# Tile 7 of a gated attention block: its normalised rows transposed by TensorE and VectorE instead of by two transposing DMAs

## The reference

```python
# x (2,1024,2048), ctx (2,2048,2048), U (2048,512), S (512), V (2048,512)
q(x, s, z) = (clip(round(x / s + z), 0, 255) - z) * s
x = x + tanh(g_xattn) * (q(layernorm(x)) @ q(ctx))
weight = (U * S) @ V.T
x = x + tanh(g_ffn) * einsum('bti,oi->bto', layernorm(x), weight)
```

## Time and profile before

| | us |
|---|---|
| median of 3 runs | 613.83 |
| the profiled execution | 616.85 |
| its span in the trace | 615.0 |
| TensorE busy | 585.1 |
| VectorE busy | 375.7 |
| ScalarE busy | 213.3 |
| GpSimd busy | 191.5 |

### The profile page before, as it was taken

How to read it: one execution, slowest core, us unless ns; L and a number is a source line. 1 busy time by engine, 2 the same in 40 slices (tenths; PEclk the granted TensorE clock), 3 DMA queues, 4 the chain that set the end, 5 groups by cost and what they waited for, 6 DMA issues and landing times.

```text
span 615.0 us, 7436 instructions
## 1 busy us (share of the span) xinstructions
PE 585.1 (95%) x2743; PEld 265.0 (43%) x2772; DVE 375.7 (61%) x694; ACT 213.3 (35%) x258; POOL 191.5 (31%) x148
## 2 busy tenths in 40 slices
PE   2899999999999999999699999999999999999997
PEld 1444444444444444444244444444444444444443
DVE  6849899994397854912363895737466564735212
ACT  5898887723050433345733310302111030301000
POOL 2898740003041438524522910040404021040000
PEclk9999999999999999999799999999999999999999
DMA  8999975539648793889974444091736436181412
GB/s 287 387 387 386 309 210 137 104 121 211 200 108 218 218 206 101 218 231 273 270 214 121 116 69 86 17 210 31 162 95 129 129 73 185 20 169 25 130 51 103
DMA packets 147844, 103.26 MB, mean 168 GB/s; under 512 B 110816, under 2 KB 110816, under 8 KB 147808
## 3 DMA queue, kind: packets, MB, share of 16 engines
q1 hardware_dynamic: 138816, 85.48, 54.0%
q10 hardware_dynamic: 8992, 17.30, 9.0%
HBM read 58.99 MB, written 16.78 MB: 123 GB/s over the span
## 4 chain that ended last, share of the span: by engine, by line
PE 59%; DMA 16%; DVE 13%; issue 4%; SPq 4%; ACT 2%; POOL 1%; ACTq 0%; DVEq 0%
PE bank L527 21%; PE bank L555 12%; DMA v_hl<-in_ctx_dram 7%; PE bank L595 6%; PE bank L600 6%; PE bank L596 6%; PE bank L560 6%; DMA xT<-xs 5%; DMA out_dram<-ring 2%; DVE ring L1067 2%; DVE u_hl L1162 2%; DVE xn L1102 2%; DMA ring<-in_x_dram 1%; DVE xs L1105 1%; DVE v_hl L1156 1%
## 5 line engine op out<-in xcount | busy, mean ns | idle before, releaser
L527 PE MATMUL bank<-q,qT 128*128 128x512 bf16 x873 | 199.1, 381 | 1.6 <-DVE ring L1067 0.3
L527 PEld LDWEIGHTS bank<-q,qT 128*128 128x128 bf16 x896 | 87.7, 98 | 107.8 <-issue 2.6
L555 PE MATMUL bank<-v_hl,xT 128*128 128x512 f16 x512 | 118.5, 386 | 6.9 <-DMA xT<-xs 6.9
L239 POOL TENSOR_SCALAR ring<-ring,bvec 128x2048 f32<-128x2048 f32 x16 | 32.8, 2051 | 271.9 <-DVE bvec L1049 271.9
L244 POOL TENSOR_TENSOR ring<-ring,corr 128x512 f32<-128x512 f32 x64 | 86.5, 1383 | 23.3 <-ACT corr L790 22.3
L595 PE MATMUL bank<-u_hl,hbuf 128*128 128x512 f16 x240 | 91.0, 379 | 2.5 <-ACT hbuf L772 1.3
L596 PE MATMUL bank<-u_hl,hbuf 128*128 128x512 f16 x240 | 91.0, 379 | 0.0
L1120 DVE SCALAR_TENSOR_TENSOR ring<-bank,cy,ring 128x512 f32<-128x512 f32 x64 | 47.3, 746 | 62.4 <-PE bank L600 62.4
L1067 DVE SCALAR_TENSOR_TENSOR ring<-bank,const,ring 128x512 f32<-128x512 f32 x64 | 47.5, 743 | 57.4 <-PE bank L527 55.0
L233 POOL TENSOR_SCALAR q<-u8r,const 128x1024 bf16<-128x1024 uint8 x52 | 64.6, 1250 | 54.6 <-ACT u8r L699 50.9
L555 PEld LDWEIGHTS bank<-v_hl,xT 128*128 128x128 f16 x512 | 50.6, 99 | 69.2 <-DMA xT<-xs 7.9
(11 more groups left out here) (119 smaller groups left out, 455.3 us busy)
## 6 DMA issues: line engine op xcount, KB each, us to landing
out_dram<-ring SPq DMA_DIRECT2D x64, 256.0 KB, 3.7
ring<-in_x_dram SPq DMA_DIRECT2D x62, 256.0 KB, 4.2
v_hl<-in_ctx_dram SPq DMA_DIRECT2D x26, 512.0 KB, 11.6
stage<-in_ctx_dram ACTq DMA_DIRECT2D x22, 512.0 KB, 5.6
q<-in_ctx_dram ACTq DMA_DIRECT2D x10, 512.0 KB, 9.5
u_hl<-in_L_ffn_V_dram SPq DMA_DIRECT2D x8, 512.0 KB, 11.5
stage<-in_ctx_dram SPq DMA_DIRECT2D x6, 512.0 KB, 11.5
stage<-in_L_ffn_U_dram SPq DMA_DIRECT2D x2, 512.0 KB, 5.8
```

Of the source, the lines that this page charges most:

```text
L527: mm = nc.tensor.matmul(unit_bank(t, n)[:, :], qT_of(t)[:, k, :], q2[:, n, k, :], start=(k == 0), stop=(k == KT - 1))
L555: nc.tensor.matmul(h_bank(u)[:, :], xT[:, g, half, k % 8, :], v_hl[:, k, 0, :], start=(g == 0 and a == 0 and half == 0), stop=False)
```

## The change

The rows of tile 7 no longer pass through the two transposing DMAs. TensorE transposes `xs` in 32 pieces of 128x128 against the identity, 8 into each bank, using banks 0 to 2 of `s1` (all of whose blocks of sequence 0 are done by then; bank 0 is used twice). VectorE copies each bank of fp16 into `xT` (`xT_copy`). On ScalarE the second half of the high part moves behind the chunks `CB+13` to `CB+15` and `hT_copy(5)`; on VectorE the second low half moves behind the last two blocks of `mm4(4)`, and `hid_lo(6)` ahead of `y_unit(5, 0)`. SyncE issues the four loads of tile 8 together.

```diff
+    X_PE = TB - 1
+        x_dma = lambda u: u + 1 - (u > X_PE)
+        x_bank = lambda g, half: bank[(2 * g + half) % 3]
...
@@ SyncE
-            load_x(8, 0)
-            x_transpose_half(7, 0)
-            load_x(8, 1)
-            x_transpose_half(7, 1)
-            load_x(8, 2)
-            load_x(8, 3)
+            for n in range(NQ):
+                load_x(8, n)
...
@@ TensorE, mm3
-                    pe.wait_ge(xT_in[g], 16 * (u + 1))
+                    if u == X_PE:
+                        pe.wait_ge(xT_copied, 2 * g + 2)
+                    else:
+                        pe.wait_ge(xT_in[g], 16 * x_dma(u))
...
+            def x_pieces(g):
+                pe.wait_ge(xs_hi, 2 * X_PE + g + 1)
+                pe.wait_ge(xs_lo, 2 * X_PE + g + 1)
+                for half in range(2):
+                    if 2 * g + half < 3:
+                        pe.wait_ge(x1_ready, S1_END(TB - 1) - (2, 1, 0)[2 * g + half])
+                    else:
+                        pe.wait_ge(xT_copied, 1)
+                    dst = x_bank(g, half)[:, :].bitcast(f16)
+                    for k in range(8):
+                        mm = nc.tensor.transpose(dst[:, k * P:(k + 1) * P], xs[:, g, half, k * P:(k + 1) * P], ident_h)
+                    mm.then_inc(xT_written, 1)
...
             h_pieces(5)
+            x_pieces(0)
             mm3(6)
+            x_pieces(1)
             mm4(5)
...
@@ ScalarE
-            x_hi(7)
+            x_hi_half(7, 0)
             stream(13, 16)
             hT_copy(5)
+            x_hi_half(7, 1)
             stream(16, 20)
...
@@ VectorE
+            def xT_copy(g):
+                for half in range(2):
+                    dve.wait_ge(xT_written, 2 * g + half + 1)
+                    dve.wait_ge(mm3_half, 2 * (X_PE - 1) + g + 1)
+                    nc.vector.tensor_copy(xT[:, g, half, :, :].rearrange("p k w -> p (k w)"),
+                                          x_bank(g, half)[:, :].bitcast(f16)).then_inc(xT_copied, 1)
...
             y_unit(4, 1)
-            x_lo_half(7, 1)
             y_unit(4, 2)
             y_unit(4, 3)
+            x_lo_half(7, 1)
+            xT_copy(0)
+            hid_lo(6)
+            xT_copy(1)
             y_unit(5, 0)
-            hid_lo(6)
             y_unit(5, 1)
```

More of the change, by code:

```diff
@@ L123, in gated_block_program @@
         hT_copied = sem("hT_copied")
+        xT_written = sem("xT_written")
+        xT_copied = sem("xT_copied")
         ident_free = sem("ident_free")
@@ L749, in x_hi_half @@
                 act.wait_ge(ln2_ready, u + 1)
-                if u > 0:
-                    act.wait_ge(xT_in[g], 16 * u)
+                if u - 1 == X_PE:
+                    act.wait_ge(xT_written, 2 * g + 2)
+                elif u > 0:
+                    act.wait_ge(xT_in[g], 16 * x_dma(u - 1))
                 nc.scalar.activation(xs[:, g, 0, :], xhalf(u, g), ACT.Identity, bias=bias, scale=scale).then_inc(xs_hi, 1)
```

## The result

The kernel after takes 607.71 us (median of 4 runs, 606.75 to 608.68), the kernel before 614.02 us beside it. The ratio is 0.9897, 95% interval 0.9868 to 0.9926: 6.3 us faster. The forecast was 604.6 us, 603.0 to 608.3, and faster. One execution of the kernel after, taken with the experiments, was slow (1051.23 us, mean granted clock 0.563) and is left out of all medians.

A forecast was written before the change was run, and what follows sets the result against it. TensorE was taken as the bound, stalled in `mm3(7)` by a transposing DMA. Terms -6.5 (stall), -3.0 (half clock), -1.3 (hidden rows), +1.8 (pieces) gave -9.0 to -9.1 us; forecast 604.6 us, range 603.0 to 608.3.

The forecast's parts named there:

- The range: Kernel time: own range 603.0 to 606.2 us with chance 0.72, widened to 608.3 for about 0.85.
- chunks as late as before: Rival: late context chunks delay `hT_copy(6)`, so `mm4(6)` waits 2.3 us; gain 6.8, 607.0 us; chance 0.15.
- The bound and the place: TensorE, 95% busy, waits 6.5 us at L555 in `mm3(7)` for the transposing DMA into `xT`.
- The price of the pieces: On TensorE, 32 added pieces cost 4 x 0.44 = 1.8 us, all on the path.
- The landing L: Landing of context chunk `CB+15`, issued at about 260.1, estimated from the room loads ahead of it: 266.5.
- The copy: VectorE's copy of a bank into `xT`: taken as 1.23 us, between 0.69 and 1.38; bank 7 margin 1.4 us.
- The clock as part of the gain: Second half of `mm3(7)`: its 16 matmuls take 6.42 us at half clock against 3.45, so 3.0 us gained.
- What is late next: `mm4(6)`, due at 296.7, needs `hT_copy(6)`, expected at about 287 instead of 297.95.
- The rival of ScalarE's queue: Part of the 0.15 rival: late `CB+15` delays ScalarE's chain; each us of landing past 267.9 costs one us.
- The sign: Profile after would show about 33.4 us from start of `mm3(6)` to start of `mm4(6)`, against 42.5 before.
- The size: Whole kernel: gain of 9.1 us, taken from the 616.85 us execution and applied to the median 613.83, giving 604.7.
- The DMA rule: By the rule the removed wait would hardly exist; the row had 20.78 us against a median 6.7 for chunk loads.

The follow-up runs named there:

- pieces_twice: Kernel after with each of the 32 transpose pieces made twice; 609.82 us, ratio to before 0.9927.
- fill14: Kernel before with 14 matmuls whose result nobody reads, placed in the stall between the halves of `mm3(7)`; 611.00 us, ratio 0.9972.
- fill26: Kernel before with 26 matmuls whose result nobody reads, placed in the stall of `mm3(7)`; 612.34 us, ratio 0.9977.
- late_half: Kernel after with ScalarE's second high half of tile 7 moved four chunks later, behind `stream(16, 20)`; 614.35 us, ratio to before 1.0011.
- before_again: Kernel before, unchanged, for a second trace and more times; 613.59 us, ratio 0.9981; its traced execution took 613.6 us.
- small_chunks: Kernel before with loads of chunks `CB+15` and `CB+20` to `CB+31` cut to a quarter of their columns, so its result is wrong; 605.48 us, ratio 0.9848.

## Why the prediction was right, and what was off

- **The range** held by luck. The forecast's own range was 603.0 to 606.2, and 607.7 lies outside it. Only the part up to 608.3, which was added for chunks as late as before, reaches it, and that did not happen: `hT_copy(6)` ran at 286.67, and nothing waited in the stretch.
- **The bound and the place** were right. The wait of L555 in `mm3(7)` was the one to remove, and 6.5 us stand in its row before, none after.
- **The price of the pieces**, 4 x 0.44 = 1.8 us on the path, was right: 2 x 0.89 us in the trace, and `pieces_twice` measures the same with twice as many. The 275 ns for a piece that the Trainium skill gives ("TensorE: Matmul & The Clock Gate", section "Part 4: PE-mode transpose") are not the price of a piece here: in a row one follows the other by 56 ns, and the clock stayed at 1.00.
- **The landing L** was put at 266.5 and came at 266.15, but the way to it was not right. It was counted from the last room load, landing at 264.5, and 1.5 us for one load more. In the trace after, the last of these, issued at 254.2, took 8.3 us and landed at 262.5, and `CB+15` took 6.2 us from its issue at 259.9. Two misses cancelled. From L on, the chain over ScalarE and VectorE was right within 0.1 us as far as `xs` (271.4, L + 5.2).
- **The copy** was mis-sized: 0.68 us instead of 1.23, at the lower of my two bounds. 1024 fp16 elements out of PSUM cost what 512 fp32 elements do in `hid_lo`, 0.69 us. It lay under cover, so with the shorter copies the margin for bank 7 was 3.1 us instead of 1.4, and the time did not change. The Trainium skill ("VectorE: DVE Perf Modes", section "The perf-mode tier table (the rule you actually need)") allows a copy out of PSUM up to twice the plain rate for 2-byte data. The trace agrees: 0.68 us, against 1.23 us for the subtraction of as many elements.
- **The clock as part of the gain** was right: the half of `mm3(7)` behind the wait takes 3.63 us in the traces of `fill14` and `fill26`, against 6.42 and 5.61. Its size is not fixed, though: 3.0 us in the first trace of before and 2.2 in the second. In the second the clock was at 0.50 from 293.0 us on and the work began at 295.41; in the first it was at 0.50 from 297.0 on and the work began at 297.89. So more of the low clock fell on idle time in the second.
- **What is late next** was right too: not `hT_copy(6)`, which was done 9 us ahead of its need. The chunks landed sooner without the two transposes. The rival of ScalarE's queue is real but needs the chunks to be some us later than they are; `late_half` shows its price.
- **The sign** "33.4 us from the start of `mm3(6)` to the start of `mm4(6)`" was worded wrongly, since 16 of the pieces stand ahead of `mm3(6)`. That distance is 264.16 to 296.58, 32.4 us; with the pieces it is 33.3.
- **The size** was off by 2.8 us, and the step is the one where the sum of 9.1 us, made in an execution of 616.85 us, was applied to the median "since neither view says where that lies". The excess lay in the stretch itself. Against an execution near the median (`before_again`) the same terms read 5.5 + 2.2 + 0.25 - 1.8 = 6.2 us, and 6.3 were measured.
- **The DMA rule** that I weighed, transposing DMAs as fast as regular ones on trn2 (the Trainium skill, "Advanced Engine Details and Errata", section "X-Bar Transpose (TRN2)"), looked refuted by 20.8 us. `small_chunks` puts it right: with less traffic beside it a transpose of 512 KB lands in 5.7 to 6.9 us, about as fast as a context chunk in the kernel after (5.7 at the median). It is the meeting of two transposes and full chunks that takes 13.7 to 21.0 us in the traces.

That the transposes' shared queue does not make them late by itself is shown by `small_chunks`, and that full chunk loads do not make a single one late is shown by the runs with one half each (7.9 to 10.3 us). It takes both, and removing either is enough. What in the engines makes the two kinds slow each other is open.

## What to carry to other kernels

A transfer's wait in one trace is a sample of something that varies. When the profiled execution lies above the median, take a second trace before carrying the whole step over: the excess may lie in the very wait that the change removes, as it did here. When a transfer is late, ask what shares the engines with it before moving its work to another engine: taking half of it away was enough here. A stall of TensorE costs its length and then the half clock behind it, so a step on another engine's queue that may bring one is dearer than its own delay.

## What was unexpected about the hardware

Useless matmuls in a wait kept the clock up and did not make the kernel slower: 12 executions with 26 of them had a mean clock of 0.999 or more, at a ratio of 0.9977. With 14, an idle of 2.25 us left the clock at 1.00 in the trace, while 5 of 12 executions of the same program show a mean clock of 0.994 to 0.997 and took 4 us more. A transposing DMA of 512 KB took 5.7 to 21.0 us, by what else was in flight.
